# A two-layer FFN and mixture kernel on one core: blank rows behind each expert's used slots, pieces of 128 and 64 rows, and short down products in rows 64 to 111

## What is computed

```python
scores = softmax(x @ gate_w.T); topk_w, topk_idx = top_k(scores, 6)   # 2048 x 6 = 12288 choices
buf = zeros((E, C, D)).at[se, pos_c].add(x[st])       # E = 64 experts, C = 384 slots each, D = 256
g = einsum('ecd,efd->ecf', buf, w_gate)               # F = 176
u = einsum('ecd,efd->ecf', buf, w_up)
eo = einsum('ecf,edf->ecd', silu(g) * u, w_down)
y = zeros_like(x).at[st].add(eo[se, pos_c] * weight)
return y + shared_swiglu(hidden)                      # and x + y at the end
```

## Time and profile before

| | busy us | share of the span |
|---|---|---|
| PE | 508.2 | 82% |
| PEld (weight loads) | 364.2 | 59% |
| POOL | 330.0 | 53% |
| DVE | 313.9 | 50% |
| ACT | 188.1 | 30% |

### The profile page before, as it was taken

How to read it: one execution, slowest core, us unless ns; L and a number is a source line. 1 busy time by engine, 2 the same in 40 slices (tenths; PEclk the granted TensorE clock), 3 DMA queues, 4 the chain that set the end, 5 groups by cost and what they waited for, 6 DMA issues and landing times.

```text
span 622.4 us, 11506 instructions
## 1 busy us (share of the span) xinstructions
PE 508.2 (82%) x2483; PEld 364.2 (59%) x2484; DVE 313.9 (50%) x823; ACT 188.1 (30%) x398; POOL 330.0 (53%) x289
## 2 busy tenths in 40 slices
PE   0797299489899899979999879999789898999920
PEld 0443153253545355558888757788668776889710
DVE  8731164274866862254445526555265544555424
ACT  0111012011221211033444425454255444455410
POOL 8900050572474767603767635655465545656750
PEclk9997689689999999989999979999799999999975
DMA  6999999996794222238999969999699989899779
GB/s 205 365 390 393 358 393 404 392 363 212 239 309 143 110 84 112 101 98 212 234 231 227 238 134 219 229 213 252 148 205 239 249 220 229 196 243 227 146 148 307
DMA packets 92394, 146.55 MB, mean 235 GB/s; under 512 B 10824, under 2 KB 72120, under 8 KB 92280
## 3 DMA queue, kind: packets, MB, share of 16 engines
q1 hardware_dynamic: 61608, 83.30, 42.6%
q0 software_dynamic: 30672, 61.75, 38.5%
HBM read 81.18 MB, written 63.83 MB: 233 GB/s over the span
## 4 chain that ended last, share of the span: by engine, by line
PE 49%; SPq 19%; DMA 10%; issue 10%; DVE 7%; POOL 3%; ACT 1%; POOLq 0%; DVEq 0%
PE bank L1074 21%; PE bank L1095 7%; PE bank L1096 7%; SPq L356 5%; SPq L355 5%; DMA x_g<-in_x 4%; PE bank L1055 4%; POOL slot_rows L491 3%; PE bank L935 2%; DMA wt<-in_wdt 2%; SPq L392 2%; PE bank L885 2%; SPq L363 2%; DVE M L749 1%; PE bank L956 1%
## 5 line engine op out<-in xcount | busy, mean ns | idle before, releaser
L502 POOL DMA_INDIRECT acc<-sil,sids x64 | 99.3, 1552 | 89.2 <-ACT sil L597 57.8
L491 POOL DMA_INDIRECT slot_rows<-ctok,sli x96 | 95.2, 991 | 80.0 <-issue 27.7
L502 POOL DMA_INDIRECT acc<-OH,sids x63 | 97.6, 1549 | 53.6 <-ACT OH L597 19.3
L1074 PE MATMUL bank<-xgT,wb 128*128 128x192 f32 (+9 forms) x384 | 85.2, 375 | 15.1 <-issue 12.8
L1074 PEld LDWEIGHTS bank<-xgT,wb 128*128 128x128 f32 (+1 forms) x384 | 65.6, 198 | 29.2 <-issue 17.0
L1096 PE MATMUL bank<-wt,hh 128*128 128x256 f32 x254 | 75.5, 379 | 0.0
L849 DVE TENSOR_TENSOR hh<-sg,bank 48x384 f32<-48x384 f32 x64 | 35.6, 556 | 74.0 <-ACT sg L586 73.2
L1096 PEld LDWEIGHTS bank<-wt,hh 128*128 128x128 f32 x254 | 48.3, 190 | 6.6
L584 ACT ACTIVATE sg<-bank 128x384 f32<-128x384 f32 x64 | 31.4, 491 | 55.4 <-PE bank L1074 55.1
L597 ACT ACTIVATE sil<-bank,wcol 128x256 f32<-128x256 f32 x64 | 29.7, 474 | 53.1 <-PE bank L1096 51.7
L597 ACT ACTIVATE OH<-bank,wcol 128x256 f32<-128x256 f32 x64 | 29.8, 474 | 51.3 <-PE bank L1096 50.0
(11 more groups left out here) (185 smaller groups left out, 739.1 us busy)
## 6 DMA issues: line engine op xcount, KB each, us to landing
cw<-slot_rows SPq DMA_DIRECT2D x127, 136.0 KB
cw<-in_cW SPq DMA_DIRECT2D x64, 256.0 KB, 6.2
wb<-in_wblk SPq DMA_DIRECT2D x32, 496.0 KB, 4.1
slot_rows<-xgT POOLq DMA_DIRECT2D x12, 1088.0 KB, 15.9
slot_rows<-wb POOLq DMA_DIRECT2D x12, 1088.0 KB, 25.0
h0T<-in_wblk SPq DMA_DIRECT2D x16, 496.0 KB
hT<-in_wblk SPq DMA_DIRECT2D x16, 496.0 KB
acc<-zrow POOLq DMA_DIRECT2D x2, 2432.0 KB
```

The source lines that it names most:

```text
L491: pool.indirect_dma_start(slots_d, bass.IndirectOffsetOnAxis(sli[:, g % 2, k, t:t + 1], 0), ctok[:, g % 2, t, :], None, bounds_check=SLOTS ...
L502: pool.indirect_dma_start(acc[u % 2], bass.IndirectOffsetOnAxis(sids[:, u % SR, j:j + 1], 0), yo[u % UE][:, j, :], None, compute_op=ALU.ad ...
L1074: ins = mm(bank[o][0:m, 0:n], w(b, c), xgT[u % UE][:, c, 0:n], start=c == 0, stop=c == DC - 1)
```

## The change

- The blank rows of the whole table go. Each expert gets 384 + 64 = 448 slots in one stretch (`SPACED`), the blocks of 16 rows and the `blk` arithmetic on DVE go, and a fourth fact `UNUSED` is the address behind the expert's used slots. SP writes 64 blank rows there from a tile `blank` (`fill`, 68 KB), eight experts ahead of the loop's load, and `loads` waits for that.
- Row counts are 64, 128, 192, 256, 320, 384 (six forms). A piece is 128 rows, the last one can be 64: in the loads, the transposes, the down products and the scatters. All engines that ask for the size now use the tree `by_rows`.
- The short down product contracts over 48 rows in place of 128 padded ones. For pieces 0 and 2 these are rows 0 to 47. For piece 1 the hidden values and the weights lie in rows 64 to 111: DVE writes that part of `hh` there (three instructions in place of one), and SP loads the 48 KB `wt` a second time for it. All long products come first, then all short ones.
- `UL` is 8, so the loop's body holds 8 experts and runs 7 times: it jumps back six times.
- PE waits for the rows ahead of the tree of `tokens`, POOL waits for pieces 1 and 2 inside its tree.

The core of the diff:

```diff
-UL = 16
+UL = 8
 LOOPS = E // UL - 1
-SIZES = [P, 3 * P // 2, 2 * P, 5 * P // 2, CAP]
+AHEAD = 1
+SIZES = [n * H for n in range(1, CAP // H + 1)]
...
+        def parts(n):
+
+            return [(j, min(P, n - j * P)) for j in range((n + P - 1) // P)]
...
             def weights(e, b):
                 sp.dma_start(wb[b], wblk[bass.ds(e, 1), :, :].rearrange("a p n -> p (a n)")).then_inc(s_wb[b], 16)
                 sp.dma_start(wt[b][0:FT], wdt[bass.ds(e, 1), :, :].rearrange("a p n -> p (a n)")).then_inc(s_wb[b], 16)
+                sp.dma_start(wt[b][CU:CU + FT], wdt[bass.ds(e, 1), :, :].rearrange("a p n -> p (a n)")).then_inc(s_wb[b], 16)
...
+            def fill(e, u):
+                sp.dma_start(slots_d[bass.ds(get(UNUSED, e, u), H), :], blank[:, :]).then_inc(s_unused[u % SR], 16)
...
-            for b in range(CAP // RB):
-                pool.dma_start(slots_d[b * E * RB:(b + 1) * E * RB, :].rearrange("(n p) c -> p n c", p=P),
-                               blanks[b % len(blanks)].unsqueeze(1).to_broadcast([P, E * RB // P, RW])).then_inc(s_init, 16)
...
-            pool.wait_ge(s_init, 16 * CAP // RB)
...
-                v.tensor_tensor(hh[0:FT, u % 2, 1, :], sg[0:FT, 1, :], bank[4][CU:CU + FT, 0:CAP], ALU.mult).then_inc(s_hh, 1)
+                for lo, hi in ((0, P), (2 * P, CAP)):
+                    v.tensor_tensor(hh[0:FT, u % 2, 1, lo:hi], sg[0:FT, 1, lo:hi], bank[4][CU:CU + FT, lo:hi], ALU.mult)
+                v.tensor_tensor(hh[CU:CU + FT, u % 2, 1, P:2 * P], sg[0:FT, 1, P:2 * P], bank[4][CU:CU + FT, P:2 * P], ALU.mult).then_inc(s_hh, 1)
...
-                        for j in range(tiles):
-                            last = tr(bank[c][:, j * P:(j + 1) * P], xg[:, u % UE, j, c * P:(c + 1) * P], ident[:, :])
+                        for j, rows in parts(n):
+                            last = tr(bank[c][:, j * P:j * P + rows], xg[0:rows, u % UE, j, c * P:(c + 1) * P], ident[0:rows, 0:rows])
...
-                    for j in (0, 2, 1)[:1 if tiles == 1 else 3]:
-                        if j < tiles:
-                            o = bank[5 + j][:, 0:D]
-                            mm(o, hh[:, u % 2, 0, j * P:(j + 1) * P], down_first(u % UE), start=True, stop=False)
-                            last = mm(o, hh[:, u % 2, 1, j * P:(j + 1) * P], wt[u % UE], start=False, stop=True)
...
+                    order = [parts(n)[i] for i in (0, 2, 1) if i < len(parts(n))]
+                    for j, rows in order:
+                        mm(bank[5 + j][0:rows, 0:D], hh[:, u % 2, 0, j * P:j * P + rows], down_first(u % UE), start=True, stop=False)
+                    for j, rows in order:
+                        lo = (j % 2) * CU
+                        last = mm(bank[5 + j][0:rows, 0:D], hh[lo:lo + FT, u % 2, 1, j * P:j * P + rows], wt[u % UE][lo:lo + FT],
+                                  start=False, stop=True)
```

More of the change, by code:

```diff
@@ L223, in program @@
         s_ws = sem("shared_weights_loaded")
-        s_init = sem("slot_tokens_initialised")
+        s_unused = [sem(f"unused_slots_filled{i}") for i in range(SR)]
         s_x = sem("x_loaded")
@@ L383, in _, with load @@
             weights(3, 3)
+            sp.wait_ge(s_const, 3)
             sp.wait_ge(s_flags, 1)
+            get, start = notes(sp, 0)
+            def fill(e, u):
+                sp.dma_start(slots_d[bass.ds(get(UNUSED, e, u), H), :], blank[:, :]).then_inc(s_unused[u % SR], 16)
+            for e in range(UE + 3 + AHEAD):
+                fill(e, e)
             for q in range(2):
                 sp.wait_ge(s_scat[q], 16 * TOPK * TG * G // 2)
-            get, start = notes(sp, 0)
             def loads(e, u):
-                def load(j):
-                    sp.dma_start(xg[:, u % UE, j, :], blocks[bass.ds(e, 1), j * P // RB:(j + 1) * P // RB].rearrange("a b r c -> (a b) r c")).then_inc(s_xg[u % UE], 16)
+                def load(n):
+                    for j, rows in parts(n):
+                        sp.dma_start(xg[0:rows, u % UE, j, :], slots_d[bass.ds(e * SPACED + j * P, rows), :]).then_inc(s_xg[u % UE], 16)
                 size = get(SIZE, e, u)
[L395 to L399, removed]
+                sp.wait_ge(s_unused[u % SR], (16 // SR) * (e - u % SR + SR))
+                sp.sem_inc(s_tick, 1)
+                by_rows(sp, size, load)
             def rows_free(e):
@@ L418, in step @@
                 if not (isinstance(e, int) and e >= E - UE - 3):
+                    if not (isinstance(e, int) and e >= E - UE - 3 - AHEAD):
+                        fill(e + UE + 3 + AHEAD, u + UE + 3 + AHEAD)
                     rows_free(e + 3)
@@ L498, in scatters, with scatter @@
             def scatters(e, u):
-                def scatter(j):
-                    pool.indirect_dma_start(acc[u % 2], bass.IndirectOffsetOnAxis(sids[:, u % SR, j:j + 1], 0),
-                                            yo[u % UE][:, j, :], None, compute_op=ALU.add).then_inc(s_acc[u % 2], 16)
+                def scatter(n):
+                    for j, rows in parts(n):
+                        if j == 1:
+                            pool.wait_ge(s_ys, 2 * e + 3)
+                            pool.wait_ge(s_yv, e + 2)
+                            pool.sem_inc(s_tick, 1)
+                        pool.indirect_dma_start(acc[u % 2], bass.IndirectOffsetOnAxis(sids[0:rows, u % SR, j:j + 1], 0),
+                                                yo[u % UE][0:rows, j, :], None, compute_op=ALU.add).then_inc(s_acc[u % 2], 16)
                 size, landed = get(SIZE, e, u), get(LANDED, e, u)
@@ L1077, in step @@
                 start(e, u)
-                by_rows(get(SIZE, e, u), gate_up)
+                by_rows(pe, get(SIZE, e, u), gate_up)
                 if not first:
```

91 lines of the change are left out of this document (36 added, 55 removed).

## The result

The changed kernel takes 708.34 us (median of 4 runs, 704.6 to 711.05) where the kernel before takes 618.94 beside it (613.84 to 621.48): a ratio of 1.145, 95% interval 1.135 to 1.155. It is slower, as forecast, but by 89 us in place of 38, and outside the range of 612 to 690. A second comparison on another chip gave 1.138 (1.128 to 1.148).

A forecast was written before the change was run, and what follows sets the result against it. Transfers were taken to bound the front and PE the loop, SP close behind. 624.1 - 31.6 (front) + 40 (shapes) + 29.6 (jumps) = 662.1; the runs' median lies 3.1 lower: 659 us, range 612 to 690.

The forecast's parts named there:

- The shape changes: PE in the expert loop: switching between full and smaller array shapes adds 40 us to the time.
- The jumps: Loop's end: six jumps back in place of two, four more at 7.4 us each, +29.6 us with nothing covering them.
- SP's added work: SP in the loop: second `wt` load, `UNUSED` read and fill per expert; taken as 0, bounds 0 to +30 us.
- The front: Before the expert loop: without the blanking, PE's and POOL's waits go, -31.6 us (28 to 35).
- The price of a shape change: PE: 0.10 us per change, plus 0.10 ahead of a full product or 0.05 ahead of transposes or 64 columns.
- The sum of 44.8 us: Loop: shape changes summed over all experts on PE; a tenth left out for stretches waiting on SP, giving 40.
- PE had no slack to hide this in: Loop: shape changes lengthen the time because PE is the bound, except in stretches where it waited for SP.
- smaller by a quarter: Loop body: fewer rows of code, still 770 rows long, so each jump still pays for a fetch.
- Rival 3: Loop: SP becomes the bound at 6.6 us per expert, 409 against 383, total 685 us; chance 0.17.
- the 383 us: PE's forecast loop time: 313 us with 40 and 30 more, or 6.1 us for each of 62 experts.
- lower half: SP's time per expert, 5.5 to 6.9 us, taken in its lower part so SP stays just below PE.
- DVE and the second `wd`: Loop: three `hh` instructions add about 0.3 us before `gate_up`, taken as 0, bound +3; second weight load counted under SP.

The follow-up runs named there:

- h1: Kernel before with contiguous fill replacing the blanking and a loop of 32 experts, each short down product cut from 128 to 48 rows; 0.965 of before, loop 318.6 us.
- h2: Kernel before with six forms in PE's trees, each short down product cut from 128 to 48 rows; 1.099 of before, loop 366.0 us.
- e1: Changed kernel with all transposes and down products back in full 128x128 shape; 703.13 us, 1.122 of before, loop 420.9 us.
- f2: Changed kernel with full 128x128 shapes and 16 experts in the loop's body (two jumps); 1.090 of before, loop 393.9 us.
- e3: Kernel before with 8 experts in the loop's body in place of 16, six jumps in place of two; 1.060 of before, loop 349.8 us.
- f1: Kernel before with both six forms in PE's trees and 8 experts in the body (six jumps); 1.128 of before, loop 389.3 us.
- e4: Kernel before with six forms in each of PE's three trees, same work; 664.56 us, 1.061 of before, loop 352.9 us.
- e2: Changed kernel with 16 experts in the loop's body in place of 8, two jumps in place of six; 1.090 of before, loop 400.8 us.
- g3: Kernel before with six forms in PE's trees and one 128-row fill per expert on SP replacing the blanking; 1.057 of before, loop 371.5 us.
- g4: Changed kernel with full shapes and a loop of 16, without the second copy of `wd` and the split `hh`; 1.081 of before, loop 385.9 us.
- e8: Kernel before with 32 experts in the loop's body, so no jump back; 0.972 of before, loop 285.9 us.
- e5: Changed kernel with SP adding the missing pieces' increments, so PE waits for a constant without reading `GATHERED`; 783.96 us, 1.117 of before.

## Why the prediction was wrong

Two steps failed. The larger trees of branches had no term, and cost 40 us. The shape changes were put on the path at 40 us, of which at most 14 are in the time. The jumps and SP's added work were taken too low.

*The front: right.* Forecast -31.6, measured -28.9 at the loop's start and -30.7 at POOL's last scatter; the groups are 38 us apart, not 36.5.

*The price of a shape change: near. Its place on the path: wrong, and the step that failed on this side.* A down of two pieces takes 1.01 + 1.20 = 2.21 us in the chain above, where it was 1.72: 0.49 more, 0.50 forecast. h1 and h2 confirm 0.30 us for a change and back. The sum of 44.8 us was somewhat high, 34 and 38 us of busy time go with the shapes in e1 and f2. That two full pieces' short products run together, and those of a 192-row expert do not, came true. But "PE had no slack to hide this in" failed. It was read from a stretch where PE was busy for 40.00 of 40 us, and the change itself made a loop in which that no longer holds: e1 and f2 show 34 and 38 us of busy time turned into 30 and 28 us of "issue" when the changes go. Of the 40 us forecast, 3 to 8 are in the loops and 0 to 14 in the ratios.

*The jumps: mechanism right, size off.* 7.4 us each were taken from two jumps; e3 measured 9.2, f1 against e4 9.1. Four are 37 us, not 29.6. Taken out of the changed kernel (e2), the four give back 24 to 28 us of loop, so there the price is lower.

*The trees: the missing term, +40.* The prediction counted rows of code ("smaller by a quarter") and used them only for the jump. Yet that quarter hides a growth: 1051 rows for 16 experts are 66 for one, 771 for 8 are 96. It said nothing of the branches within an expert, which step over the forms not taken. e4 shows their price with nothing else changed. The trace of before held a hint that I didn't use: line 1074 stood for 18.5 us on "issue", and the two jumps of the earlier trace rows are only 9.3.

*SP: 0 taken, about 19 measured with a fill of 128 rows (g3)*, within the bounds of 0 to +30. SP itself is hardly in the chain (1% of it in the page of after), yet the fill lengthens the loop. Rival 3 did not happen as a bound on SP's queue, but it was near. SP's loop without its waits is 424.4 - 26.2 = 398 us, 6.4 for each expert, above the 383 us and the "lower half" of 5.5 to 6.9 that the prediction took. By that (an estimate), SP would have been the bound had PE kept to 383.

*DVE and the second `wd`: 0 taken, +3 as bound for DVE, 8 measured together (g4), and the waits ahead of the branches 2 to 5.* The latter does not stand out from the 4 us between two traces of one kernel, and the 8 hardly do.

The parts now sum to 312.9 + 37 + 40 + 19 + 8 + 4 = 421, and 3 to 8 for the shapes that remain visible (after against e1, e2 against f2): 424 to 429, where the two traces have 424.4 and 428.6. The close fit should not be trusted, for the parts were measured on different kernels and chips, most by one trace each. The direction was right by luck. By the prediction's own terms the front and the jumps cancel (-31.6 + 29.6), and "slower" hung on the 40 us for the shapes, few of which are in the time. What made the kernel slower were the jumps at 37 us, the trees at 40, and SP.

What is the cause beneath the trees and the jumps? "Issue" means only that no semaphore was waited for. In the traces it goes with the packets of queue 8: 64, 70, 82, 89, 98 and 107 of them have loops of 286, 313, 350, 353, 389 and 424 us (e8, before, e3, e4, f1, after; g3, f2 and e2 lie 4 to 19 us above the row, with 89, 98 and 98). The branches show it one by one. Of those over 0.5 us, the last packet of queue 8 had landed 1.3 to 1.6 us ahead of the branch's end in all 16 of before, all 39 of e4, all 43 of f1 and in 34 of the 37 of after. Of the branches under 0.3 us, 5 to 8 in a hundred lie in that distance. So PE's long branches are waits for code: this the traces show. That "issue" comes from them is shown in part. Gaps that touch a long branch or begin within 0.6 us behind it hold 11 of the 22 us of "issue" in the loop of before, 26 of 52 in e4, 62 of 79 in f1 and 44 of 70 in after. So the jumps' price is such waiting for the most part. For the trees of e4, 15 of the 30 us are; the rest may be gaps that open later, when what the sequencer had issued ahead is used up, and that is not shown.

The Trainium skill, Runtime: NRT & Kernel Launch, section Instruction fetch mechanics, says that code comes in blocks of 16 KB by the engine's own queue and that a taken branch whose target lies outside the blocks held waits for a fetch. By that each form stepped over moves a target further away, and the traces agree, in the packets' number and in the landings. The 35 us that the changed kernel's loop takes over f1's are not such waits, of which f1 has more (92.6 us against 77.2).

## What to carry to other kernels

Count the code of each form, not only the work in it: doubling the forms of branches inside a loop cost 40 us on this kernel with the same work, and a jump back 9. Count rows for one expert and not for the whole body, when the unrolling changes too. Price a finer tiling as new forms plus shape changes (0.30 us for one and back), and take it only if what it saves on the engine that bounds is more; here 64-row pieces saved PE nothing. When an edit relieves an engine and the time stays, look whether another one has just become the bound, as SP did in e5. Separate the parts of a change that gain from those that lose: the fill that replaces the blanking, with fewer jumps in place of more, makes this kernel 8% faster (571.6 us against 622.3).

## What the runs showed of the hardware

- A 48-row product between full ones makes the distance from product to product 0.52 to 0.63 us in place of 0.43 (h1). Over a whole kernel the busy time shows the price in full (37 us for 127). The time shows 27 to 29 us of it in h1, 13 (by the loops) to 24 (by the ratios) in h2, and in f2 against e2 7 us in the loop and nothing in the ratio.
- Two 48-row products of 128 columns of weights each, in rows 0 to 47 and 64 to 111, started 7 ns apart; with 64 columns in the second they did not overlap (four matmuls in 0.70 against 1.27 us, after).
- Most branches of PE took 0.07 to 0.22 us. Those over 0.5 us, up to 6.0 in the changed kernel, ended 1.3 to 1.6 us behind the landing of a 16 KB instruction packet in 98 of 98 cases of before, e4 and f1.
- Costs of an engine's instruction stream and of its array are not additive: taking array time away gave back 30 us as "issue" (e1).
- The same kernel took 619 to 627 us on four chips and 695 and 702 on two others, with a stretch of the front where SP's transfers are issued at 2.6 us each. The fill brought the loop's start forward by 27 to 34 us on the first kind and by 19 to 23 on the second.
